# Splitting the first gathering product of each cell of a two-layer graph convolution into two of 64 edges

## What is computed

```python
def gcn_conv(x, W, b, src, dst, n):
    h = x @ W
    deg = jnp.zeros((n,), h.dtype).at[dst].add(1.0) + 1.0
    dinv = jax.lax.rsqrt(deg)
    norm = dinv[src] * dinv[dst]
    agg = jax.ops.segment_sum(h[src] * norm[:, None], dst, num_segments=n)
    return agg + h * (dinv * dinv)[:, None] + b

h = gcn_conv(emb, W1, b1, src, dst, NTOKEN)
nodes = gcn_conv(h, W2, b2, src, dst, NTOKEN)
return nodes[input.reshape(-1)].reshape(b_, l_, NINP)
```

## Time and profile before

| | |
|---|---|
| Median of 2 runs | 4070.93 us (4069.74 to 4072.11) |
| Span of the profiled execution | 3584.7 us |
| Difference, which lies outside the span | 486.2 us |
| TensorE busy in the span | 2691.2 us, 75% |
| VectorE busy | 3038.2 us, 85% |
| GpSimd busy | 1801.4 us, 50% |
| ScalarE busy | 1368.1 us, 38% |

### The profile page before, as it was taken

How to read it: one execution, slowest core, us unless ns; L and a number is a source line. 1 busy time by engine, 2 the same in 40 slices (tenths; PEclk the granted TensorE clock), 3 DMA queues, 4 the chain that set the end, 5 groups by cost and what they waited for, 6 DMA issues and landing times.

```text
span 3584.7 us, 76006 instructions
## 1 busy us (share of the span) xinstructions
PE 2691.2 (75%) x28220; PEld 2486.1 (69%) x28220; DVE 3038.2 (85%) x8759; ACT 1368.1 (38%) x3173; POOL 1801.4 (50%) x1609
## 2 busy tenths in 40 slices
PE   6999443442126799999999997899999999999000
PEld 5887222321126788999999997899999999999000
DVE  9999999999976899999999997688889988898100
ACT  5776221221134344444444443344444444444000
POOL 2000000000016656676767664576777777777776
PEclk9999555665558999999999999999999999999555
DMA  3000000000013333344344444455555434444130
GB/s 86 0 0 0 18 13 14 18 13 9 0 41 77 88 90 85 92 100 98 95 99 96 97 97 111 123 157 153 156 154 158 95 97 95 100 96 97 26 26 12
DMA packets 205828, 267.52 MB, mean 75 GB/s; under 512 B 100083, under 2 KB 112668, under 8 KB 205214
## 3 DMA queue, kind: packets, MB, share of 16 engines
q1 hardware_dynamic: 154364, 188.88, 18.3%
q0 software_dynamic: 51136, 74.26, 12.1%
HBM read 211.50 MB, written 52.45 MB: 74 GB/s over the span
## 4 chain that ended last, share of the span: by engine, by line
PE 50%; DVE 37%; POOL 7%; issue 3%; DMA 1%; ACT 1%; SPq 1%; POOLq 0%; DVEq 0%
PE ps L1132 18%; PE ps L1197 18%; PE ps L1014 9%; DVE oh L1756 8%; DVE keys L1445 7%; DVE keys L1446 6%; DVE keys L1661 4%; POOL out L877 3%; PE ps L1163 2%; DVE zoh L1740 2%; POOL arena L864 2%; POOL zring L800 1%; PE ps L1168 1%; PE ps L1080 1%; DVE arena L1667 1%
## 5 line engine op out<-in xcount | busy, mean ns | idle before, releaser
L800 POOL DMA_INDIRECT zring<-table,sidx x1298 | 1485.3, 1144 | 642.9 <-issue 313.2
L968 ACT ACTIVATE steps_oh<-ps 128x384 bf16<-128x384 f32 x1912 | 938.7, 491 | 1280.1 <-PE ps L1132 1274.2
L1132 PE MATMUL ps<-arena,keys 128*128 128x192 bf16 x11472 | 1268.4, 247 | 53.7 <-DVE oh L1756 25.2
L1197 PE MATMUL ps<-steps_oh,oh 128*128 128x192 bf16 x11466 | 1269.9, 247 | 0.0
L1132 PEld LDWEIGHTS ps<-arena,keys 128*128 128x128 bf16 x11472 | 980.0, 98 | 61.9 <-DVE oh L1756 31.5
L1756 DVE TENSOR_SCALAR oh<-io_h,dl 128x384 bf16<-128x384 int16 x3822 | 998.2, 321 | 15.3 <-PE ps L1197 14.7
L1197 PEld LDWEIGHTS ps<-steps_oh,oh 128*128 128x128 bf16 x11466 | 980.6, 98 | 5.8 <-issue 0.3
L1661 DVE TENSOR_SCALAR keys<-keys,lanes 128x1024 bf16<-128x1024 int16 x1434 | 613.7, 481 | 29.2 <-DMA keys<-srel 17.4
L721 POOL DMA_INDIRECT arena<-line,row_i x16 | 15.9, 992 | 1036.3 <-DVEq L1516 1032.1
L1080 PE MATMUL ps<-ident,keys 128*128 128x128 f32 x464 | 102.5, 415 | 308.2 <-DVE keys L1446 303.2
L1740 DVE TENSOR_SCALAR zoh<-io_h,dl 128x128 bf16<-128x128 int16 x1064 | 243.7, 263 | 90.0 <-PE ps L1197 86.7
(11 more groups left out here) (281 smaller groups left out, 1725.9 us busy)
## 6 DMA issues: line engine op xcount, KB each, us to landing
keys<-srel SPq DMA_DIRECT2D x478, 256.0 KB
out<-res SPq DMA_DIRECT2D x50, 512.0 KB
zring<-table,sidx POOLq DMA_INDIRECT x1298
table<-arena SPq DMA_DIRECT2D x19, 384.0 KB, 2.8
table<-sgn_l SPq DMA_DIRECT2D x39, 144.0 KB
nodes<-arena SPq DMA_DIRECT2D x39, 96.0 KB
arena<-in_L_rec_edge_index SPq DMA_DIRECT2D x2, 1171.5 KB, 6.6
out<-arena,oidx POOLq DMA_INDIRECT x110, 2.2
```

The lines of the kernel that those rows point to most:

```text
L800: pool.indirect_dma_start(out=zring[:, i % RING, :], out_offset=None, in_=rows_of, in_offset=bass.IndirectOffsetOnAxis(ap=sidx[:, col:col ...
L968: act.activation(grow[:, j % 2, h * 2 * ROW:(h + 1) * 2 * ROW], pg[h][:, 0:2 * ROW], ACT.Copy).then_inc(evac, 1)
L1132: mm = pe.matmul(pg[t // 2][:, t % 2 * ROW:(t % 2 + 1) * ROW], s_oh[:, j // 2 % 2, k, e:e + P], xtab[:, (w * WIN + k) * ROW:(w * WIN + k + ...
L1197: mm = pe.matmul(sums(sl, k), dwin[:, j % 2, t, k * P:(k + 1) * P], grow[:, j % 2, t * ROW:(t + 1) * ROW], start=False, stop=(w == CELLS - ...
```

## The change

The first of the three gather products of each cell (k = 0) becomes two: one with the first 64 columns of the one-hot matrix, which writes PSUM partitions 0 to 63, and one with the other 64, which writes partitions 64 to 127. Each streams the same 192 columns of `xtab`. For each half batch the four small products of its two cells come first, then the four full ones (k = 1, 2 of both cells). The flag `start` is set on the small products of the half's first cell alone, and everything else adds. `gmm` is still raised by the last product of the half. Nothing changes on the other engines.

```diff
-                def gather(j, t, k):
-                    w = (j * BT + t) % CELLS
-                    e = (j % 2 * BT + t) * P
-                    table_to(w * WIN + k)
-                    mm = pe.matmul(pg[t // 2][:, t % 2 * ROW:(t % 2 + 1) * ROW], s_oh[:, j // 2 % 2, k, e:e + P],
-                                   xtab[:, (w * WIN + k) * ROW:(w * WIN + k + 1) * ROW], start=(k == 0), stop=(k == WIN - 1))
-                    if t % 2 and k == WIN - 1:
-                        mm.then_inc(gmm, 1)
+                def gather(j, h):
+                    for t in (2 * h, 2 * h + 1):
+                        w = (j * BT + t) % CELLS
+                        e = (j % 2 * BT + t) * P
+                        table_to(w * WIN)
+                        for half in range(2):
+                            pe.matmul(pg[h][half * 64:(half + 1) * 64, t % 2 * ROW:(t % 2 + 1) * ROW],
+                                      s_oh[:, j // 2 % 2, 0, e + half * 64:e + (half + 1) * 64],
+                                      xtab[:, w * WIN * ROW:(w * WIN + 1) * ROW], start=(t % 2 == 0), stop=False)
+                    for t in (2 * h, 2 * h + 1):
+                        w = (j * BT + t) % CELLS
+                        e = (j % 2 * BT + t) * P
+                        for k in range(1, WIN):
+                            table_to(w * WIN + k)
+                            mm = pe.matmul(pg[h][:, t % 2 * ROW:(t % 2 + 1) * ROW], s_oh[:, j // 2 % 2, k, e:e + P],
+                                           xtab[:, (w * WIN + k) * ROW:(w * WIN + k + 1) * ROW], start=False,
+                                           stop=(t % 2 == 1 and k == WIN - 1))
+                    mm.then_inc(gmm, 1)
...
-                            for t in (2 * h, 2 * h + 1):
-                                for k in range(WIN):
-                                    gather(j + 1, t, k)
+                            gather(j + 1, h)
```

More of the change, by code:

```diff
@@ L1202, in _ @@
                 pe.wait_ge(s_ready, layer * NPAIR + FREE + 1)
-                for t in range(BT):
-                    for k in range(WIN):
-                        gather(0, t, k)
+                for h in range(2):
+                    gather(0, h)
                 for j in range(NB):
```

## The result

| | median, us | range |
|---|---|---|
| before | 4070.93 | 4069.74 to 4072.11 |
| changed | 4228.82 | 4227.78 to 4229.87 |

The changed kernel is slower: ratio 1.0405, 95% interval [1.0383, 1.0428], +158 us where +334 was forecast. But its profiled execution has a span of 4228.1 us, all but the whole of its time (its run took 4229.9). That of the kernel before spanned 3584.7 us, 486 under its runs. So the first question is what these 486 us are; the prediction had them outside the span.

What follows compares the result with a forecast made beforehand. TensorE's stream was taken as the bound before and after. Its terms, 54 + 0 + 356 = 410 us, less 76 us of waits, gave 334 us more: 4070.9 + 334 = 4405 us, range 4085 to 4730 us.

Steps and rivals of the forecast that it cites:

- What bounds: Both layers' loops: TensorE's stream of products sets the pace, before and after the change.
- Term 1: Small gather products: the two halves overlap, the second an issue step behind, paid once per group of four; 54 us.
- B: Small products: halves don't overlap and width changes are free; 238 us more, 4309 us, chance 0.19.
- D: Small products: no overlap and a drain at width changes; 4665 us, or 4978 with the full drain; chance 0.16.
- Term 2: Loads of 64 stationary columns: hidden by the slot, taken as 0, with bounds of 0 and 84 us.
- Term 3: Passages between full and half width, two a half batch: half of a product's 165 ns under its successors, plus load; 356 us.
- free passage of the earlier trace: In the sort, going from 128 output partitions to 1 cost nothing; taken as the passage's lower bound.
- A: Small products: halves overlap and passages are free; say 4095 us, not slower by 2%; chance 0.22.
- C: Small products: halves overlap, with a full drain of 0.175 us a passage; 647 us more, 4718 us, chance 0.11.
- What hides: In the loops, 76 us of TensorE's 105 us of waits for VectorE cover added work; two single waits are left out.
- the forecast's signs: Changed profile: both windows 0.17 us a half batch longer, TensorE's waits on VectorE near zero, VectorE some 80% busy.
- the last of the sum: Whole run: the span, forecast at 3919 us, stays 486.2 us under the median, so 334 us are added to 4070.9.

Runs made afterwards that it cites:

- quick chips: Four of the five chips of the later runs: the kernel before takes 3587 to 3591 us there, the changed kernel 3906.3 us (ratio 1.0882).
- all-small kernel: Changed kernel with all gather and scatter products split into half-width pairs: 3722.5 us on a quick chip (ratio 1.0363 to the kernel before), 4271.9 on the late chip.
- kernel before with hold-ups: Kernel before plus an idle VectorE reduction in every eighth batch, 120 in all: 3987.8 us on a quick chip (ratio 1.111), 4389.9 on the late chip.
- late chip: The fifth chip of the later runs: the kernel before takes 4071 us there, as in the first comparison, and semaphore signals come late in its traces.
- hold-ups of 3.35 us: Changed kernel plus an idle VectorE reduction in every eighth batch, 120 in all: 4294.2 us on a quick chip, ratio 1.196 to the kernel before.
- those of 1.15 us: Changed kernel plus a shorter idle VectorE reduction in every fourth batch, 238 in all: 3985.1 us on a quick chip, ratio 1.1102 to the kernel before.

## Why the prediction was wrong

By its steps, with the quick chips' numbers:

- **What bounds: right.** Both loops are TensorE's after the change (98% and 100% busy), and the added time is in them.
- **Term 1, the halves overlap: right, and the size too, for another reason.** They start 3 ns apart, and a group of two pairs takes 28 ns over one slot (3 + 104 + 3 against 82), 1912 x 0.028 = 54 us as forecast. The reason given, an issue step behind the first half, is worth 3 ns; the rest are the 24 ns of the first pair, once a group. That 28 was forecast and 28 measured is luck. Rivals B and D fall.
- **Term 2, the loads: right at zero in a row, not at the head of one.** The all-small kernel leaves no room for a cost of 64-column loads behind each other. The Trainium skill's page "TensorE: Matmul & The Clock Gate", section "Weight-path perf modes", keeps the fast load for 128 columns. The trace agrees as far as it goes: 64-column loads are recorded 108 ns long and 128-column ones 98; they hide in a row. Where they don't run ahead, at the head of a row, they cost the 24 ns of term 1.
- **Term 3, the passage: right.** 94 ns in and 96 ns out were measured, and 10 more to the next full product, which the forecast counted too: 382 us for 356. That half of the 165 ns came so close is luck as much as judgement. The free passage of the earlier trace rows was not a guide. The rule of the Trainium skill's page "TensorEngine Tiling (Array Packing)", section "Key Properties", holds in this trace: a change of mode costs those 94 and 96 ns, and tiles of one mode run in parallel, 3 ns apart. Rivals A and C fall.
- **What hides: more.** 434 us (54 + 382, less rounding) - 317 = 117 us for 76. TensorE's stops in the loops (distances of over 0.21 us between two starts, less one slot) sum to 156 us in 214 places before and 46 us in 56 after, 110 less. The forecast took the idle time for VectorE alone, 105 us, and left out two waits. But in each stop most of the last product's 165 ns pass as busy time, in which nothing new starts, and these go with the wait. TensorE's waits for VectorE fell to 32 us, and both windows grew by 0.17 us a half batch, as the forecast's signs had it.
- **The failed step is the last of the sum:** "it lies 486.2 us under the median of the runs, and I keep that". The span and the time of one execution are the same to 2 us in every run. The 486 us were no constant outside the span but a difference between two executions under different conditions. For the changed kernel 300 of its 323 us lie in the loops, for the kernel before with hold-ups 381 of 406; for the kernel before itself there is no trace. What the late chip adds is no constant either: 323 us to the changed kernel, 486 to the one before, 549 to the all-small one. So +334 on 3588 would have been near (3922 forecast by its span, 3906 measured), while 4071 + 334 was not, with +158 measured. Why the late chip has its late signals, and what sets how much of them a kernel pays, stays open; that room on the other engines shortens their effect is shown for short hold-ups of VectorE only.
- **A slip without effect on the sum:** the range is said to leave out most of rival D, but D's first time, 4665 us, lies in it.

## To carry to other kernels

Compare the profiled span with the runs before adding anything to either: where they are far apart, as 3585 and 4071 us were here, the trace and the times are of different conditions, and a sum made on the trace can't be moved to the times. In this kernel two products with outputs on half of the partitions cost as much as one full one if they come in long rows of their own kind, and each change to or from full width cost a little more than a full product of 192 columns (94 to 106 ns against 82); so group them over as many cells as the banks allow, or leave the width alone. Idle time of an engine doesn't cover a hold-up longer than its lead: the changed kernel paid 388 of 402 us with hold-ups of 3.35 us, and 79 of 274 with those of 1.15 us.

## What was not expected

- One pair alone has a dearer way out than two: 203 ns after the last small product, against 178. It is no cost of its own: the first pair is 24 ns longer than the second in every group, and with one pair these stand in the way out.
- Nothing was gained anywhere: the best of the split kernels that do the whole work, all small, is 3.6% behind the kernel before, which stays the quickest.
- The same program takes 3588 us on some chips and 4071 us on another, 13% apart, with the runs of each set within 0.6% of their median. The stages up to 1065 us take the same on both, though the engines hand off to each other there too. The loops and the lookup at the end are longer. In both GpSimd fetches or writes rows by index all the time, and up to 1036 us it does not; whether that is the reason no run tests.
